# A GNN + MoE layer: the weighted sum over neighbour rows moves its factors and its accumulator into PSUM

## What is computed

```
x = x + gnn(layernorm(x));   x = x + ffn(layernorm(x))

gnn: feat_all = einsum('ni,rhid->rnhd', inputs, conv_weights)      # 8 types, 4 heads of 64
     el = sum(feat_all[type, src] * attn_l[type]);  er = sum(feat_all[type, dst] * attn_r[type])
     e = leaky_relu(el + er, 0.2)
     ex = exp(e - segment_max(e, dst)[dst]);  alpha = ex / segment_sum(ex, dst)[dst]
     h = segment_sum(alpha * feat_all[type, src], dst) + h_bias
ffn: probs = softmax(x @ gate_w + gate_b);  cw = the two largest of the 8, else 0
     out = sum over experts of cw[e] * (gelu(x @ W1[e] + b1[e]) @ W2[e] + b2[e])
```

## Time and profile before

| | |
|---|---|
| median of the runs | 2616.04 us (2614.4 to 2618.78) |
| span of the profiled execution | 2256.0 us |
| median less span | 360.0 us |
| POOL busy | 1504.5 us (67%) |
| PE busy | 1390.8 us (62%) |
| DVE busy | 1210.3 us (54%) |
| ACT busy | 643.8 us (29%) |
| mean granted share of PE's clock | 0.812 |
| windows 0 to 29: first node rows, scores of window 29 | 422.27, 2109.98 us |

### The profile page before, as it was taken

One profiled execution on the slowest core, in us unless ns is written; L12 is line 12 of the kernel. 1 busy time (PEld: TensorE's weight loads), 2 busy tenths in 40 slices (PEclk: granted clock), 3 DMA queues, 4 the chain that ended last, 5 costly groups with the idle time before them and its releaser, 6 DMA issues.

```text
span 2256.0 us, 26567 instructions
## 1 busy us (share of the span) xinstructions
PE 1390.8 (62%) x7174; PEld 1112.0 (49%) x7174; DVE 1210.3 (54%) x2282; ACT 643.8 (29%) x2351; POOL 1504.5 (67%) x1213
## 2 busy tenths in 40 slices
PE   2637994016877766676766676656666455465456
PEld 1313441006767665666656565555565354465344
DVE  5413004146767656655656565665666454567462
ACT  3212331013443333333333232332333321223121
POOL 1604113388888888878888888888888887888530
PEclk9878997557999888888887878788888777786677
DMA  5462333743333333333333333333333333323210
GB/s 152 155 161 75 128 134 136 208 123 88 86 83 81 90 88 90 88 90 87 87 92 82 90 85 86 84 85 87 86 86 84 92 89 97 85 80 82 67 37 3
DMA packets 113692, 214.93 MB, mean 95 GB/s; under 512 B 58478, under 2 KB 70357, under 8 KB 109510
## 3 DMA queue, kind: packets, MB, share of 16 engines
q0 software_dynamic: 57936, 153.93, 25.8%
q1 hardware_dynamic: 38688, 25.68, 4.3%
q10 hardware_dynamic: 16892, 33.82, 4.0%
HBM read 172.86 MB, written 44.87 MB: 97 GB/s over the span
## 4 chain that ended last, share of the span: by engine, by line
POOL 56%; issue 17%; PE 3%; POOLq 2%; DVE 2%; ACT 0%; DMA 0%; DVEq 0%; ACTq 0%; SPq 0%
POOL rows L873 52%; PE y_ps L1436 1%; POOL node_row L890 1%; POOL out_dram L881 1%; PE hid_ps L1422 1%; POOL xrows L873 1%; POOLq L886 1%; POOLq L921 1%; POOLq L792 0%; DVE xrows L1084 0%; DVE xrows L1088 0%; DMA xrows<-table,idx_x 0%; ACT hT L1332 0%; POOLq L909 0%; DVE xo L1177 0%
## 5 line engine op out<-in xcount | busy, mean ns | idle before, releaser
L873 POOL DMA_INDIRECT rows<-table,idx_st x1014 | 1294.8, 1277 | 309.0 <-issue 308.7
L1436 PE MATMUL y_ps<-w,hT 128*128 128x256 f32 (+1 forms) x1920 | 526.6, 432 | 530.5 <-ACT hT L1332 514.4
L1436 PEld LDWEIGHTS y_ps<-w,hT 128*128 128x128 f32 (+1 forms) x1920 | 401.3, 216 | 624.3 <-ACT hT L1332 545.6
L1422 PE MATMUL hid_ps<-zT,w 128*128 128x128 f32 (+1 forms) x3840 | 486.8, 287 | 0.0
L1422 PEld LDWEIGHTS hid_ps<-zT,w 128*128 128x128 f32 x3840 | 472.9, 202 | 17.5 <-ACT hT L1332 11.2
L1332 ACT ACTIVATE hT<-hid_ps,b1t 128x128 f32<-128x128 f32 (+1 forms) x960 | 268.6, 370 | 251.7 <-PE hid_ps L1422 249.4
L1025 DVE TENSOR_TENSOR rows<-rows 128x2080 f32<-128x2080 f32 x106 | 246.2, 2322 | 20.4 <-ACT rows L1342 14.6
L1020 DVE TENSOR_TENSOR rows<-rows,ex 128x2080 f32<-128x2080 f32 (+1 forms) x136 | 256.1, 1902 | 1.6
L983 DVE TENSOR_TENSOR score<-score,rows 128x160 f32<-128x160 f32 x30 | 9.7, 325 | 457.5 <-SPq L838 395.9
L586 PE MATMUL feat_ps<-wc,xnT 128*125 128x512 f32 x480 | 230.7, 627 | 37.2 <-ACT xnT L519 25.1
L1311 ACT ACTIVATE th<-e_diff 128x160 f32<-128x160 f32 x30 | 10.1, 336 | 735.9 <-DVE e_diff L1001 735.9
(11 more groups left out here) (172 smaller groups left out, 974.5 us busy)
## 6 DMA issues: line engine op xcount, KB each, us to landing
table<-stage ACTq DMA_DIRECT2D x30, 1031.2 KB
rows<-table,idx_st POOLq DMA_INDIRECT x1014, 2.8
w<-in_L_ffn_W_dram SPq DMA_DIRECT2D x16, 512.0 KB, 14.3
blocks<-edge_row SPq DMA_DIRECT2D x1, 4351.5 KB, 54.2
x_all<-in_x_dram SPq DMA_DIRECT2D x3, 1250.0 KB
node_tab<-x_all SPq DMA_DIRECT2D x3, 1250.0 KB
wc<-_L_gnn_conv_weights_dram ACTq DMA_DIRECT2D x16, 128.0 KB, 6.7
attnb<-in_L_gnn_attn_l_dram SPq DMA_DIRECT2D x1, 1024.0 KB, 10.8
```

What stands on the lines that cost most here:

```text
L873: q.indirect_dma_start(buf[:, k, :], None, table, bass.IndirectOffsetOnAxis(idx[:, col + k:col + k + 1], 0)).then_inc(landed, 16)
L1422: last = t.matmul(hid_ps[e % 2][:, m * P:m * P + n], w1[:, e, k, m * P:(m + 1) * P], zT[:, k, 0:n], start=(k == 0), stop=(k == KD - 1))
L1436: last = t.matmul(y_ps[p % 2][0:n, (e % 2) * D:(e % 2 + 1) * D], hT[e % 2][:, k, 0:n], w2[:, e, k, :], start=(k == 0), stop=(k == KH - 1))
```

## The change

- The bank of `agg_ps` and one more become `fold_ps`, 1024 numbers a partition in PSUM. It holds three lanes of 260 (`lanes`), a second copy of the numerators (`ex_ps`, 160), and `er9` for both buffers (72). DVE now clears `er9`, not POOL.
- `exps` computes the numerators twice, into `ex` (for ACT) and into `ex_ps` (for DVE).
- `weigh_all` multiplies slots 0 to 2 by `ex_ps` straight into the lanes, slots 3 to 11 and 12 to 20 in place. ACT has slots 21 to 31. Above degree 32 DVE also weights slots 32 to 39.
- In place of the folds, `add` adds three slots at a time to the three lanes. At the end a copy and two additions bring the lanes together in `acc`.
- PE's `sums` and `agg_ok` are gone. A group is given back to POOL by `freed`, in the order 0, 1, 2, 3, and POOL gathers in that order.

```diff
-    BY_ACT = 7
+    LANES = 3
+    ACT_LO, ACT_HI = 21, 32
-    N_FRONT, N_EX, N_BEGIN, N_POST, N_GATE, N_MIX = 6, 6, 5, 16, 11, 1 + NE
+    N_FRONT, N_EX, N_BEGIN, N_POST, N_GATE, N_MIX = 6, 18, 5, 16, 11, 1 + NE
-    er9 = [sb(f"er9{i}", [P, H, R1]) for i in range(2)]
-    agg_ps, gate_ps, zt_ps = bank("agg_ps"), bank("gate_ps"), bank("zt_ps")
+    gate_ps, zt_ps = bank("gate_ps"), bank("zt_ps")
+    fold_ps = env["ctx"].enter_context(nc.psum_tensor("fold_ps", [P, 1024], F32))
+    lanes = fold_ps[:, 0:LANES * AGG].rearrange("p (k c) -> p k c", k=LANES)
+    at = LANES * AGG
+    ex_ps = fold_ps[:, at:at + H * NS].rearrange("p (h k) -> p h k", h=H)
+    at += H * NS
+    er9 = [fold_ps[:, at + i * H * R1:at + (i + 1) * H * R1].rearrange("p (h r) -> p h r", h=H) for i in range(2)]
...
-            for n, s in enumerate((1, 3, 2, 0)):
+            for s in range(PAIRED):
                 if not isinstance(w, int) or w >= 2:
-                    if s:
-                        pool.wait_ge(folded, (w - 2) * 3 + (n + 1))
-                    else:
-                        pool.wait_ge(agg_ok, w - 1)
+                    pool.wait_ge(freed, (w - 2) * PAIRED + (s + 1))
...
             st.did(v.tensor_scalar(ex[:], rden[:], 2.0, -1.0, ALU.mult, ALU.add))
+            st.did(v.tensor_scalar(ex_ps, rden[:], 2.0, -1.0, ALU.mult, ALU.add))
...
+        def weighted(par, lo, hi, out=None):
             r = rows[par][:, lo:hi, 0:AGG].rearrange("p k (h c) -> p k h c", h=H)
+            o = r if out is None else out.rearrange("p k (h c) -> p k h c", h=H)
+            return v.tensor_tensor(o, r, bc(ex_ps[:, :, lo:hi].rearrange("p h k -> p k h"), 3, HC), ALU.mult)
+
+        def add(par, lo, n=LANES):
+            return v.tensor_tensor(lanes[:, 0:n], rows[par][:, lo:lo + n, 0:AGG], lanes[:, 0:n], ALU.add)
...
-            st.did(weighted(par, 0))
+            st.did(weighted(par, 0, LANES, lanes))
+            st.did(weighted(par, LANES, 12))
             for _ in range(2):
                 next(gate, None)
-            st.did(weighted(par, 1))
+            st.did(weighted(par, 12, ACT_LO))
...
             with dve.If(degree > PAIRED * SLOTS):
-                weighted(par, PAIRED)
+                weighted(par, PAIRED * SLOTS, NS)
                 dve.drain()
-                fold(par, 0, PAIRED)
-                dve.drain()
-            fold(par, 0, 1).then_inc(folded, 1)
+                for lo, n in ((32, 3), (35, 3), (38, 2)):
+                    add(par, lo, n)
+                    dve.drain()
+            for lo in (3, 6):
+                st.did(add(par, lo))
+                st.wait()
+            dve.sem_inc(freed, 1)
             for _ in gate:
                 pass
-            st.did(weighted(par, 2))
-            st.did(weighted(par, 3, BY_ACT))
-            st.wait()
+            for lo in (9, 12, 15):
+                st.did(add(par, lo))
+                st.wait()
+            dve.sem_inc(freed, 1)
+            st.did(add(par, 18))
+            between()
             dve.wait_ge(act_weighed, w + 1)
-            fold(par, 2, 3).then_inc(folded, 1)
-            between()
-            dve.wait_ge(folded, w * 3 + 2)
-            fold(par, 0, 2).then_inc(folded, 1)
+            st.wait()
+            st.did(add(par, 21))
+            st.wait()
+            dve.sem_inc(freed, 1)
+            for lo in (24, 27):
+                st.did(add(par, lo))
+                st.wait()
+            st.did(add(par, 30, 2))
+            st.wait()
+            dve.sem_inc(freed, 1)
+            st.did(v.tensor_copy(acc_f, lanes[:, 0]))
+            st.wait()
+            st.did(v.tensor_tensor(acc_f, acc_f, lanes[:, 1], ALU.add))
+            st.wait()
+            v.tensor_tensor(acc_f, acc_f, lanes[:, 2], ALU.add).then_inc(acc_ok, 1)
...
-                weigh(w, par, 0, 3)
+                weigh(w, par, 21, 25)
                 gelu(u, 2)
-                weigh(w, par, 3, 5)
+                weigh(w, par, 25, 29)
                 gelu(u, 3)
-                weigh(w, par, 5, BY_ACT)
+                weigh(w, par, 29, ACT_HI)
...
-            sums(w, par)
```

More of the change, by code:

```diff
@@ L673, in phase2 @@
     acc = sb("acc", [P, H, HC])
+    acc_f = acc[:].rearrange("p h c -> p (h c)")
     r4 = sb("r4", [P, H])
@@ L718, in phase2 @@
     y_ps = [bank(f"y_ps{i}") for i in range(2)]
-    agg_ps, gate_ps, zt_ps = bank("agg_ps"), bank("gate_ps"), bank("zt_ps")
+    gate_ps, zt_ps = bank("gate_ps"), bank("zt_ps")
[5 more added lines that the diff above has]
+    er9 = [fold_ps[:, at + i * H * R1:at + (i + 1) * H * R1].rearrange("p (h r) -> p h r", h=H) for i in range(2)]
+    assert at + 2 * H * R1 <= 1024
     b2_ps = zt_ps[:, 256:256 + D]
@@ L735, in phase2 @@
     act_weighed = sem("act_weighed")
-    folded = sem("folded")
-    agg_ok = sem("agg_ok")
+    freed = sem("freed")
     acc_ok = sem("acc_ok")
@@ L864, in _ @@
         q = nc.gpsimd
-        for i in range(2):
-            q.memset(er9[i][:], MASKED).then_inc(const_ok, 1)
         bt = Batches(pool, "pool")
@@ L977, in scores @@
             st.wait()
-            st.did(v.tensor_tensor(eh, bc(er9[par][:], 1, n), bc(hot, 2, H), ALU.mult))
+            st.did(v.tensor_tensor(eh, bc(er9[par], 1, n), bc(hot, 2, H), ALU.mult))
             st.wait()
@@ L1039, in weigh_all @@
             with dve.If(degree > PAIRED * SLOTS):
-                weighted(par, PAIRED)
+                weighted(par, PAIRED * SLOTS, NS)
                 dve.drain()
-                fold(par, 0, PAIRED)
-                dve.drain()
-            fold(par, 0, 1).then_inc(folded, 1)
+                for lo, n in ((32, 3), (35, 3), (38, 2)):
[5 more added lines that the diff above has]
+            dve.sem_inc(freed, 1)
             for _ in gate:
                 pass
-            st.did(weighted(par, 2))
-            st.did(weighted(par, 3, BY_ACT))
-            st.wait()
-            dve.wait_ge(act_weighed, w + 1)
-            fold(par, 2, 3).then_inc(folded, 1)
-            between()
-            dve.wait_ge(folded, w * 3 + 2)
-            fold(par, 0, 2).then_inc(folded, 1)
-            assert st.n == N_EX
+            for lo in (9, 12, 15):
[4 more added lines that the diff above has]
+            between()
+            dve.wait_ge(act_weighed, w + 1)
+            st.wait()
+            st.did(add(par, 21))
[11 more added lines that the diff above has]
+            st.wait()
+            assert st.n == N_EX, st.n
+            v.tensor_tensor(acc_f, acc_f, lanes[:, 2], ALU.add).then_inc(acc_ok, 1)
         def take(w):
-            dve.wait_ge(agg_ok, w + 1)
-            v.tensor_copy(acc[:], agg_ps[:, 0:AGG].rearrange("p (h c) -> p h c", h=H)).then_inc(acc_ok, 1)
             dve.wait_ge(acc_ok, w + 1)
@@ L1267, in _ @@
         dve.sem_inc(cleared, 1)
+        for i in range(2):
+            v.memset(er9[i], MASKED).then_inc(const_ok, 1)
         dve.wait_ge(const_ok, 2)
@@ L1335, in weigh @@
         def weigh(w, par, lo, hi):
-            if lo == 0:
+            if lo == ACT_LO:
                 act.wait_ge(ex_step, w * N_EX + 2)
-            for k in range((PAIRED - 1) * SLOTS + lo, (PAIRED - 1) * SLOTS + hi):
+            for k in range(lo, hi):
                 for h in range(H):
@@ L1342, in weigh @@
                     last = a.activation(r, r, ACT.Copy, scale=ex[:, h, k:k + 1])
-            if hi == BY_ACT:
+            if hi == ACT_HI:
                 last.then_inc(act_weighed, 1)
@@ L1366, in window @@
             else:
-                weigh(w, par, 0, BY_ACT)
+                weigh(w, par, ACT_LO, ACT_HI)
             nb, g = bt.enter(w)
@@ L1446, in b2_term @@
             t.matmul(b2_ps, cwT[:], b2s[:], start=True, stop=True).then_inc(b2_ok, 1)
[L1448 to L1453, removed]
-            last.then_inc(agg_ok, 1)
         def window(w, par, half):
```

6 lines of the change are left out of this document (removed).

## The result

The changed kernel takes 2793.02 us (median of 4 runs, 2786.93 to 2797.44); the kernel before, run beside it, 2615.6 us. The ratio is 1.067, 95% interval 1.0645 to 1.0694: slower by 177 us, where 268 us less were forecast.

The account below looks back on a forecast made before the run. POOL, its gathers held by DVE instructions with two SBUF inputs, was taken as the bound; freeing them, with longer DVE chains, gave 269 us, less 1 us at the end, so 2616.0 became 2348 us; 80% range 2295 to 2430 us.

Parts of the forecast that it names:

- work around it that is not changed: 360 us between the profile's span of 2256.0 us and the runs' median of 2616.0 us, taken as outside the span.
- POOL issues back to back: From the first window to the last, POOL waits for nobody before 1014 gathers, so it sets each window's length.
- the rivals: POOL stays bound, 2297 us, 7%; PSUM half rate, 2775 us, 5%; every long DVE instruction holds gathers, about 2645 us, 3%.
- the holds that I called a brake: DVE instructions with two SBUF inputs hold up POOL's gathers: mean 1290 ns in windows 1 to 13, in place of 945.
- The slower rival: Writing or re-reading an accumulator in PSUM goes at half rate: +159 us, 2775 us; chance 5%, writes alone another 5%.
- Gathers at 1.25 us with the gap: On POOL, a gather that nothing holds takes 0.95 us, 1.25 us with the gap.
- PSUM at SBUF's rate: DVE's instructions on PSUM run at the same rate, 1.044 ns an element: additions of 780 elements take 0.96 us.
- the copy at 429 ns: DVE reading 260 elements out of agg_ps takes 429 ns against 421 in SBUF, so reading PSUM costs no time.
- The gain of 269 us: Whole span: 9 us before window 1, then 83, 64, 84 and 29 us in the four stretches, together 269 us.
- my forecast: Windows of 44.3, 48.0, 51.8 and 58.3 us in the four stretches; the row gives the saving against before.
- POOL's term: On POOL, gathers no longer held: 1.25 us each with gap; windows 1 to 13 need 40.5 us each, not 50.7.
- DVE's term: DVE's loop round a window grows by 5.1 to 5.3 us, to 44.3, 48.0, 48 and 58.0 us in four stretches.

Follow-up runs that it names:

- e0: The kernel before, unchanged, run and profiled again: 2584.42 us, span 2582.6 us.
- e7: The kernel before with a drain on POOL before every eighth gather: 2620.29 us, ratio 1.0134 to the kernel before.
- e2: The changed kernel with accumulator lanes, ex_ps and er9 in SBUF in place of PSUM: 2599.98 us, ratio 0.994 to the kernel before.
- e9: The changed kernel with accumulator, numerators and er9 in SBUF and a drain before every eighth gather: 2555.16 us, ratio 0.9875 to the kernel before.
- e5: The changed kernel with a drain on POOL before every eighth gather: 2376.2 us, ratio 0.9064 to the kernel before; once more 2380.97 us, ratio 0.9201.
- e10: The changed kernel with each gather fetching 264 bytes a row in place of 1056: 2786.03 us, ratio 1.0773 to the kernel before.
- e8: The changed kernel with a drain on POOL before every sixteenth gather: 2554.33 us, ratio 0.9898 to the kernel before.
- e12: The changed kernel with a 200-byte memset before each gather of rows and one drain a window: 2549.97 us, ratio 0.987 to the kernel before.
- e6: The changed kernel with twelve register additions on POOL before each gather, no drain: 2798.36 us, ratio 1.0657 to the kernel before.
- e1: The changed kernel with a small memset and a drain on POOL before every gather: 4575.29 us, ratio 1.7707 to the kernel before.
- e11: The changed kernel with a drain on POOL before every twelfth gather: 2432.74 us, ratio 0.9397 to the kernel before.

## Why the prediction was wrong

- **The failed step.** "The profile gives no other time of its own execution; the runs' median of 2616.0 us is 360 us above that span, work around it that is not changed." There is no such work: in all 13 runs with a profile of their own the span lies 1.7 to 1.8 us below the run's time (e0: 2582.6 and 2584.26). The 360 us are late signals inside the windows, which the profiled execution lacked and each timed one seems to have had (e0 has them, and its 10 runs lie within 0.4%). Everything that followed was worked out for a course the timed runs do not take.
- **What bounds.** "POOL issues back to back" is true of the 2256 us execution and of e7. In e0, POOL waits, and its chain share is 5%. There the faster gathers win little.
- **What takes the time.** A mechanism that none of the rivals named. With the holds gone, the trains get unbroken: 236 gathers above 1.5 us in the trace of 2256.0 us, 132 in e0, 90 in e2, 2 after. So the holds that I called a brake also kept the trains from harming (e2 against the changed kernel). How is not shown: few of the late signals come through inside a train beside a held gather (5 of the 145 remote waits above 5 us in e0 and e2). The slower rival (PSUM at half rate, 2775 us) came near the measured time by accident: additions take 973 ns.
- **Durations.** Gathers at 1.25 us with the gap, PSUM at SBUF's rate, the copy at 429 ns: all as forecast. The Trainium skill, page "VectorE: DVE Perf Modes", section on the TRN2 errata, would have put each PSUM instruction some 65 ns higher; the copy out of PSUM at 429 ns and 780 elements at 973 ns (forecast without it 0.96 us) show at most 15 ns of it.
- **The holds.** The inference on the page "SBUF — State Buffer" of the Trainium skill, section "Who interferes with whom", that `tensor_tensor` leaves descriptor generation alone, fails a second time: e9 and e5 differ by the place of one tile, and the gathers by 1131 against 951 ns.
- **The gain of 269 us.** With drains in both kernels, where the unknown releaser has under 1% of the chain, the change wins 239 us (2620.29 to 2380.97). The table has us a window by the starts of the scores; the last two rows are differences, of e7 less e5 and of my forecast:

```
windows          1-13   14-19   20-26   27-28
before (2256)    50.7    58.6    63.8    73.0
e0               62.6    71.8    78.4    66.1
after            69.6    76.7    83.5    85.4
e7               60.4    72.9    76.6    88.2
e5               54.4    60.9    67.2    78.3
e7 - e5           6.0    12.0     9.4     9.9
forecast          6.4    10.6    12.0    14.7
```

So the gain came near in size once both programs ran without late signals on the chain, and POOL's term is borne out (1217 against 951 ns a gather, 270 us over 1014). DVE's term is not: in windows 1 to 13 of e5 DVE waits 0.3 us a window for its rows, and a round takes 54.4 us where 44.3 were forecast. Drains and 8 us a window of ACT's remaining remote waits are in that, so what the DVE chain takes alone is open, and the agreement of the two gains is in part luck. The sum was set against the wrong course of the program. That the same 269 us would have come off the 2256.0 us execution is argued, not shown: no execution of the changed kernel without drains had prompt signals.

What stays open is why a train does this. It is not bytes (e10) and not the length of the program (e2). The slow register instructions narrow it down. The number of DVE's `ALU_OP` records over 0.6 us, of 1301 in the kernel before and 1651 in the others:

```
2256.0 us execution   0        e8 (drain every 16)   35
e0                    5        e12 (even spacing)    63
after               354        e6 (registers)       369
e1 (far apart)        0        e10 (short rows)     352
e2 (SBUF)            18        e7 (before, drains)    0
e5 (drain every 8)    1        e9 (SBUF, drains)      0
e11 (every 12)       33
```

They are gone where the gathers are far apart or the trains are cut to eight, and they wait for no semaphore, so a slow path for semaphores alone does not explain them: the sequencer itself is held. In e0 they are few though its signals are late, so there may be more than one effect. Whether it is the gathers' writes of their descriptors, a path that semaphores and sequencers share, or the recording of events itself was not tried. The Trainium skill, page "NOTIFIC — the notification-queue block", section "Overflow: three behaviours, one of which stalls the engine", says that the block which records events always holds back its producers when its inner queues fill. A sequencer that is held would fit that, but no run here shows or excludes it, since each timed execution carries the same record of spans; if it is so, a part of the effect goes with the recording. Why the kernel before once ran without late signals is open too. Late signals leave DVE idle, idle DVE holds fewer gathers (132 against 236), and fewer holds mean longer trains, so both courses could feed themselves; this is argued from counts only.

## What to carry to other kernels

Compare the span of the profiled execution with the runs' time before reading anything else. Here 13 pairs differ by 1.7 to 1.8 us and one by 360; that one shows another course of the program, and its bound was not the bound of the time. Idle time of a busy engine can be worth keeping: where a long train of gathers runs beside a chain of small steps that hand over between engines, try a break every eight or so, and judge any edit that makes gathers faster together with the breaks: drains won 412 us on the changed kernel and lost 1.3% on the kernel before.

## What the hardware showed that was not expected

- A drain between gathers costs 2.6 us over the ordinary gap (2.9 to 3.1 against 0.30 us idle), and most of the waiting signals get through in it (36 of 40 waits above 5 us in e5).
- In a train, ACT waits for PE's signals up to 9.3, 15.0, 18.5 and 37.2 us, as the train gets longer. DVE's steps of 0.15 us come 1.40 us apart in its late part, and the register instructions between them, which wait for nothing, take 0.70 us in place of 0.04.
- Twelve register additions on POOL between two gathers cost nothing measurable (gap 0.3 us in both).
